# Layer 0 of a feature-interaction tower: products of pairs on VectorE in five of 32 units, in place of sums on TensorE and squares on ScalarE

## The reference: what is computed

```
xk = x0
for W in (W0, W1, W2):
    xk = relu(einsum('bmd,bhd,mhk->bkd', x0, xk, W))   # products of every field with every row of xk
    outs.append(sum(xk, axis=2))                        # over d
z = concatenate(outs, axis=1)                           # (1024, 192)
h = relu(concatenate([z, dense_ctx]) @ W_top1 + b_top1); h = relu(h @ W_top2 + b_top2); y = h @ W_top3
```

## Time and profile before

| | |
|---|---|
| median of 3 runs | 628.99 us (628.71 to 633.98) |
| the profiled execution, its own time | 630.75 us |
| its span, first to last instruction | 629.0 us |
| TensorE / VectorE / GpSimd / ScalarE busy | 606.1 / 514.3 / 444.0 / 322.1 us |
| clock granted to TensorE, mean | 0.997 of full |

### The profile page before, as it was taken

The page is one execution under the profiler, slowest core; times in us unless marked ns, Lnnn a source line. Parts: engine busy times, 40 slices in busy tenths (PEclk is TensorE's granted clock), DMA queues, the critical chain, the costliest instruction groups (busy, mean ns, idle before and its releaser), DMA issues.

```text
span 629.0 us, 8379 instructions
## 1 busy us (share of the span) xinstructions
PE 606.1 (96%) x2884; PEld 210.1 (33%) x2884; DVE 514.3 (82%) x454; ACT 322.1 (51%) x539; POOL 444.0 (71%) x346
## 2 busy tenths in 40 slices
PE   2788999999999999999999999999999999999998
PEld 1522333333333333333333333333333333333354
DVE  0058499999989998999999998999899998888600
ACT  1225546564636465564556463646546455643554
POOL 6777577878787878788787878787887876456400
PEclk9998999999999999999999999999999999999999
DMA  4886877877776768777678777677776767750000
GB/s 128 288 286 219 285 253 259 284 254 281 268 264 215 281 235 266 262 247 259 235 280 282 277 245 256 221 278 266 254 258 248 263 246 279 268 160 35 1 0 1
DMA packets 45199, 144.49 MB, mean 230 GB/s; under 512 B 9619, under 2 KB 24085, under 8 KB 32870
## 3 DMA queue, kind: packets, MB, share of 16 engines
q1 hardware_dynamic: 36966, 141.85, 62.3%
q0 software_dynamic: 8192, 2.11, 3.1%
HBM read 139.21 MB, written 4.72 MB: 229 GB/s over the span
## 4 chain that ended last, share of the span: by engine, by line
PE 95%; ACT 2%; DMA 1%; SPq 1%; DVE 1%; issue 0%; DVEq 0%
PE acc L658 68%; PE acc L650 13%; PE x_ps L624 5%; PE x_ps L691 2%; PE sums_ps L691 2%; PE acc L636 2%; DMA w_sb<-in_w 1%; PE acc L710 1%; ACT x_ps L520 1%; DVE dve_ring L579 1%; PE sums_ps L698 1%; PE acc L638 0%; ACT pair_squares L501 0%; PE sums_ps L705 0%; PE sums_ps L624 0%
## 5 line engine op out<-in xcount | busy, mean ns | idle before, releaser
L579 DVE TENSOR_TENSOR dve_ring<-x_wide,x_ps 128x1024 f32<-128x1024 f32 x428 | 488.2, 1212 | 62.1 <-issue 39.5
L658 PE MATMUL acc<-dve_ring,w_sb 128*64 128x512 f32 x1712 | 492.2, 595 | 5.8 <-DVE dve_ring L579 5.8
L460 POOL DMA_INDIRECT gathered<-in_table,idx x256 | 243.9, 953 | 69.6 <-issue 63.6
L472 POOL TENSOR_TENSOR pool_ring<-x_wide,x_sb 128x1024 f32<-128x1024 f32 x84 | 199.1, 2379 | 81.4 <-ACT x_sb L529 48.3
L658 PEld LDWEIGHTS acc<-dve_ring,w_sb 128*64 128x64 f32 x1712 | 155.1, 137 | 294.7 <-issue 273.4
L650 PE MATMUL acc<-pool_ring,w_sb 128*64 128x512 f32 x336 | 139.5, 592 | 0.0
L636 PE MATMUL acc<-pair_squares,w_sb 128*64 128x512 f32 x256 | 115.7, 592 | 2.4 <-ACT pair_squares L501 2.4
L520 ACT ACTIVATE x_ps<-acc 64x512 f32<-64x512 f32 x128 | 73.0, 570 | 77.9 <-PE acc L658 64.4
L524 ACT ACTIVATE layer_out<-acc 64x512 f32<-64x512 f32 x96 | 56.5, 588 | 60.3 <-PE acc L658 35.8
L501 ACT ACTIVATE pair_squares<-x_ps 128x1024 f32<-128x1024 f32 x32 | 32.8, 1026 | 98.3 <-PE sums_ps L624 98.3
L529 ACT COPY x_sb<-layer_out 64x512 f32<-64x512 f32 x128 | 79.0, 617 | 3.6
(11 more groups left out here) (36 smaller groups left out, 131.3 us busy)
## 6 DMA issues: line engine op xcount, KB each, us to landing
x_wide<-x_rows SPq DMA_DIRECT2D x96, 1024.0 KB, 7.8
x_wide<-x_rows SPq DMA_DIRECT2D x32, 768.0 KB, 5.6
x_wide<-x_rows SPq DMA_DIRECT2D x32, 256.0 KB
gathered<-in_table,idx POOLq DMA_INDIRECT x256, 5.4
x_rows<-gathered SPq DMA_DIRECT2D x32, 128.0 KB, 2.3
w_sb<-in_w SPq DMA_DIRECT2D x2, 512.0 KB, 5.1
x_rows<-gathered SPq DMA_DIRECT2D x32, 16.0 KB, 2.6
x_wide<-in_W_top SPq DMA_DIRECT2D x1, 512.0 KB, 6.4
```

Source lines behind the costliest of these rows:

```text
L460: pool.indirect_dma_start(gathered[:, c, j % 2, e * DIM:(e + 1) * DIM], None, table, bass.IndirectOffsetOnAxis(ap=idx[:, unit, e:e + 1], a ...
L472: nc.gpsimd.tensor_tensor(pool_ring[:, c], x0_step(c, j, layer, 2 * d, 2).rearrange("p (s n) -> p s n", n=COLS), x_sb[:, layer - 1, c, :]. ...
L579: nc.vector.tensor_tensor(dve_ring[:, c, slot:slot + width, :], x0_step(c, j, layer, i, width).rearrange("p (s n) -> p s n", n=COLS), x_ps ...
L658: done = nc.tensor.matmul(a, w, dve_ring[:, c, n % DVE_RING + i - at, :], start=first, stop=last)
```

## The change

Five units, (0, 4), (0, 6), (0, 8), (0, 10) and (0, 12), named `BY_PRODUCTS`, make their layer 0 otherwise. Their `sums` burst and the two squares of it are left out. SP loads a fifth operand for them, the *partners* (128 x 512, 256 KB): partition 4m+q holds field m+4+12q. It lands in the last tile of `pair_squares`. VectorE then multiplies the first four steps of `x0_wide` by the partners in one instruction of 128 x 2048 (`pairs`), both operands in SBUF, and writes the four tiles of `pair_squares`. Those are the products of all pairs. TensorE's five steps of layer 0 stay, with other weights (`w0p_sb`, summed at the start from two arrays, and `w0p_diag`). ScalarE still squares the fields by themselves. For the same five j GpSimd takes one more double of layer 2 of thread 1: doubles 2 and 5 in place of 5 alone.

```diff
+PARTNER, PARTNER_APART = 4, 12
+BY_PRODUCTS = frozenset((0, j) for j in range(4, 14, 2))
...
-    return {1: (6,), 2: ((3, 7), (5,))[c]}[layer]
+    return {1: (6,), 2: ((3, 7), (2, 5) if (0, j) in BY_PRODUCTS else (5,))[c]}[layer]
...
+def pairs_slot(c, j):
+    return begin(c, j) + 6
...
# pe_order
-            works.append((sum_slot(c, j) + 0.5, "sums", c, j + 1, 0, 0))
+            if (c, j + 1) not in BY_PRODUCTS:
+                works.append((sum_slot(c, j) + 0.5, "sums", c, j + 1, 0, 0))
# dve_order
+        if (c, j + 1) in BY_PRODUCTS:
+            works.append((pairs_slot(c, j), "pairs", c, j + 1, 0, 0, 0))
# sp_order
             works.append((at + 30, "block", c, j + 2, 0))
+            if (c, j + 2) in BY_PRODUCTS:
+                works.append((at + 32, "partners", c, j + 2, 0))
             works.append((at + 34, "block", c, j + 2, 1))
...
+            def load_partners(c, j):
+                rows = rows_of(c, j)
+                sp.wait_ge(layer0_done[c], j)
+                sp.dma_start(partner_steps(c),
+                             bass.AP(rows.tensor, rows.offset + PARTNER * COLS,
+                                     [[COLS, FIELDS], [PARTNER_APART * COLS, Q], [1, COLS]])).then_inc(partners_loaded[c], 16)
...
+            sp.dma_start(w0p_sb[:], w0_near).then_inc(pair_weights, 16)
+            sp.dma_start(w0f_sb, w0_far).then_inc(pair_weights, 16)
+            sp.dma_start(w0p_diag[:], w0_diag).then_inc(pair_weights, 16)
...
# GpSimd, ahead of its loop
             pool.wait_ge(w0_summed, 1)
+            pool.wait_ge(w0_added, 2)
...
# ScalarE, squares
+                if (c, j) in BY_PRODUCTS:
+                    act.wait_ge(layer0_done[c], j)
+                else:
+                    act.wait_ge(sums_made, sums_before(c, j) + 4)
                     bank = sum_banks(c, j)
                     nc.scalar.activation(pair_squares[:, c, 0:2, :], x_ps[:, bank:bank + 2, :],
                                          ACT.Square).then_inc(squares_made, 1)
                     nc.scalar.activation(pair_squares[:, c, 2:4, :], sums_ps[:], ACT.Square).then_inc(squares_made, 1)
...
+            def pairs(c, j):
+                wait_first_step(dve, c, j)
+                wait_block(dve, c, j, 0)
+                dve.wait_ge(partners_loaded[c], 16 * (products_before(c, j) + 1))
+                dve.wait_ge(layer0_done[c], j)
+                nc.vector.tensor_tensor(
+                    pair_squares[:, c],
+                    x0_step(c, j, 1, 0, SUM_TILES).rearrange("p (s n) -> p s n", n=COLS),
+                    partner_steps(c).unsqueeze(1).broadcast_to([P, SUM_TILES, COLS]),
+                    ALU.mult).then_inc(pairs_made[c], 1)
...
# VectorE, ahead of its loop
+            dve.wait_ge(pair_weights, 48)
+            nc.vector.tensor_tensor(w0p_sb[:], w0p_sb[:], w0f_sb, ALU.add).then_inc(w0_added, 1)
...
# TensorE, layer0
+                if by_products and i == 0:
+                    pe.wait_ge(pairs_made[c], products_before(c, j) + 1)
+                if by_products and i == SUM_TILES:
+                    pe.wait_ge(squares_made, squares_before(c, j) + 1)
...
-            pe.wait_ge(w0_added, 2)
+            pe.wait_ge(w0_added, 3)
```

More of the change, by code:

```diff
@@ L118, in dve_groups, with squares_before, sums_before, products_before @@
     return [(i, 2) for i in range(0, STEPS, 2) if not by_pool(c, j, layer, i)]
+def pairs_slot(c, j):
+    return begin(c, j) + 6
+def squares_before(c, j):
+    return sum(1 if (d, n) in BY_PRODUCTS else 3 for n in range(j + 1) for d in range(THREADS) if (n, d) < (j, c))
+def sums_before(c, j):
+    return sum(4 * ((d, n) not in BY_PRODUCTS) for n in range(j + 1) for d in range(THREADS) if (n, d) < (j, c))
+def products_before(c, j):
+    return sum((c, n) in BY_PRODUCTS for n in range(j))
+def squares_of_sums(c, j):
+    return 0 if (c, j) in BY_PRODUCTS else squares_before(c, j) + 1
 def mlp_plan():
@@ L230, in cin_tower @@
 def cin_tower(nc, dense_ctx, ids, base, table, w_top1, b_top1, w_top2, b_top2, w_top3,
-              w0_ab, w0_ba, w0_diag, in_pair, of_field, w1, w2, ident, out):
+              w0_ab, w0_ba, w0_diag, w0_near, w0_far, in_pair, of_field, w1, w2, ident, out):
     with ExitStack() as ctx:
@@ L258, in cin_tower @@
         w0d_sb = sb("w0d_sb", [P, HK])
+        w0p_sb = sb("w0p_sb", [P, SUM_TILES, HK])
+        w0p_diag = sb("w0p_diag", [P, HK])
         in_pair_sb = sb("in_pair_sb", [P, P])
@@ L273, in cin_tower @@
         of_field_sb = pool_ring[:, 0, 1, :].rearrange("p (t n) -> p t n", n=P)
+        w0f_sb = pool_ring[:, 1, 1, 0:SUM_TILES * HK].rearrange("p (t k) -> p t k", k=HK)
         dense = pool_ring[:, 1, 0, 0:TILES * DIM].rearrange("p (t f) -> p t f", f=DIM)
@@ L303, in cin_tower @@
         weights_b = sem("weights_b")
+        pair_weights = sem("pair_weights")
         w0_added = sem("w0_added")
@@ L314, in cin_tower @@
         squares_made = sem("squares_made")
+        partners_loaded = sems("partners_loaded")
+        pairs_made = sems("pairs_made")
         dve_made = sems("dve_made")
@@ L430, in _ @@
                     stage(c, j)
+                elif work == "partners":
+                    load_partners(c, j)
                 elif work == "block":
@@ L510, in finish @@
                 wait_layer(act, layer, c, j)
[L512 to L517, removed]
+                if layer == 0 and c == 0 and j > 0 and squares_of_sums(1, j):
+                    act.wait_ge(squares_made, squares_of_sums(1, j))
+                if layer == 0 and c == 1 and 0 < j < UNITS - 1 and squares_of_sums(0, j + 1):
+                    act.wait_ge(squares_made, squares_of_sums(0, j + 1))
+                if layer == 1 and j < UNITS - 1 and (c, j) != (0, 0) and squares_of_sums(c, j + 1):
+                    act.wait_ge(squares_made, squares_of_sums(c, j + 1))
                 if layer < 2:
@@ L601, in _ @@
                     product(c, j, layer, i, width)
+                elif work == "pairs":
+                    pairs(c, j)
                 else:
@@ L628, in layer0 @@
                 a = acc[j % 2][out_half(c), :]
[L629 to L634, removed]
+                if i == 0 and j > 1:
+                    pe.wait_ge(out_made[2][c], j - 1)
+                by_products = (c, j) in BY_PRODUCTS
+                if by_products and i == 0:
+                    pe.wait_ge(pairs_made[c], products_before(c, j) + 1)
+                if by_products and i == SUM_TILES:
+                    pe.wait_ge(squares_made, squares_before(c, j) + 1)
+                if not by_products and i != 1:
+                    pe.wait_ge(squares_made, squares_before(c, j) + (1, 0, 2, 2, 3)[i])
                 if i < SUM_TILES:
-                    nc.tensor.matmul(a, w0_sb[:, i, :], pair_squares[:, c, i, :], start=(i == 0), stop=False)
-                else:
-                    nc.tensor.matmul(a, w0d_sb[:], own_squares[:, c, :],
+                    w = (w0p_sb if by_products else w0_sb)[:, i, :]
+                    nc.tensor.matmul(a, w, pair_squares[:, c, i, :], start=(i == 0), stop=False)
+                else:
+                    w = w0p_diag if by_products else w0d_sb
+                    nc.tensor.matmul(a, w[:], own_squares[:, c, :],
                                      start=False, stop=True).then_inc(layer0_done[c], 1)
@@ L744 @@
         arrays[name] = tiles
+    m, t, q = np.meshgrid(np.arange(FIELDS), np.arange(SUM_TILES), np.arange(Q), indexing="ij")
+    near, far = (m + Q_APART * q + t) % FIELDS, (m + PARTNER + PARTNER_APART * q) % FIELDS
+    twice = ((far - near) % FIELDS == FIELDS // 2) & (near > far)
+    for name, (first, second) in (("w0_near", (near, far)), ("w0_far", (far, near))):
+        tiles = np.where(twice[..., None], np.float32(0), w0[first, second])
+        arrays[name] = tiles.transpose(0, 2, 1, 3).reshape(P, SUM_TILES, HK)
     arrays["of_field"] = np.zeros((P, SUM_TILES, P), np.float32)
```

24 lines of the change are left out of this document (11 added, 13 removed).

## The result

The change makes the kernel slower by 0.6%: 634.45 us as the median of 18 runs (632.27 to 637.00) against 631.03 for the kernel before (628.10 to 633.98, 18 runs), a ratio of 1.0059 with a 95% interval of 1.0040 to 1.0078. That is +3.4 us where -5.4 was forecast, and above the range.

A forecast was written before the change was run, and what follows sets the result against it. TensorE bounds the kernel, VectorE 1.3 to 2.4 us short of it. Five bursts at -1.23 us plus 0.7 given back make -5.4 us: 625.3 for the profiled execution, median 623.6, range 622.5 to 632.

The forecast's parts named there:

- the duration of the pair products: VectorE, 128 x 2048 from SBUF: 2.26 us long, next product 2.16 us after; a second SBUF operand costs nothing by itself.
- the first rival: VectorE's pair products and GpSimd's doubles wait for each other; chance 0.27 for (a), 0.12 for (b).
- case (a): VectorE gets its turn after GpSimd's first double: 1.6 lost against 1.23 gained, sum +1.4, 630.4 us; chance 0.27.
- the sign that its mechanism is wrong: In the profile after, TensorE waiting at all five places; a wait of about 0.7 us was expected at unit (0,4) alone.
- thread 0 half a slot behind thread 1: TensorE's order of steps: (0,9) step 14 taken nine slots after the burst, thread 0 half a slot behind.
- What is removed: TensorE's five bursts of sums, 5 x 1.23 = 6.2 us; the squares on ScalarE give nothing.
- VectorE's leads: VectorE's products behind the pair products: (1,8) step 12 keeps 0.65 us, (0,9) step 14 keeps 0.55, so no stall.
- GpSimd's two doubles: Start at 357.75 behind three gathers, end at 360.1 and 362.5, 0.75 and 0.55 us in hand: costs nothing.
- The first unit: Unit (0,4), VectorE has no double less: products come 2.16 us later, TensorE waits some 0.7 us, given back.
- The additional double: GpSimd's new double runs to 354.1, before TensorE takes step 4 at about 355.7: in time.
- the loads: Partners there by about 356, before 358.55; thread 1's near rows land at 369.2, before its burst at 370.4: nothing.

The follow-up runs named there:

- e1: Changed kernel with the pair products of all five units 5.5 slots later, behind GpSimd's two doubles; 628.38 us, ratio 0.9973 to the kernel before.
- e7: e6 with GpSimd's additional doubles two units earlier, so the first unit with pair products has one ahead too; 624.49 us, ratio 0.9892 to the kernel before.
- e6: e1 with one GpSimd gather moved behind its double for step (1,j,1,12) in the units of the pairs; 624.81 us, ratio 0.9891 to the kernel before.
- e3: Kernel before with only GpSimd's additional double in thread 1's units 4, 6, 8, 10 and 12; 631.02 us, ratio 1.0026 to the kernel before.
- e2: Changed kernel without GpSimd's additional double, pair products at their old slot; 630.96 us, ratio 1.0020 to the kernel before.

## Why the prediction was wrong

**The failed step** is the duration of the pair products. "I take 2.16" was right for the work (2.28 alone; 2.26 was worked out) and wrong for the place: in the change VectorE's next product starts 365.01 - 361.33 = 3.68 us after them. The argument that reads of a second SBUF operand cost nothing rested on a sum of 256 columns which, as the prediction itself says, met no double of GpSimd. It told nothing about the one condition that mattered, and "the rows neither show such a wait nor exclude it" should not have left the forecast ahead of the rival. The Trainium skill, "SBUF — State Buffer", section "Who interferes with whom", says that a VectorE instruction with two SBUF inputs contends with a GpSimd instruction that reads SBUF, and that the one issued later blocks. This case agrees: 1.60 us until the first double ended, 2.2 us for the second until the pair products ended, and neither in e1. That the second SBUF operand is the reason is not tried by itself, since no run moves an operand; what speaks for it is that VectorE's products with one operand in PSUM read the same `x0_wide`, ran beside the same doubles, and never took over 1.24 us in any of these kernels. The rule and the overlap of the two (358.55 inside 357.75 to 360.1, in the prediction's own schedule) were both in hand.

**What happened is the first rival, case (a),** with VectorE's turn between the two doubles. The order of the turns, the steps that wait and the signs were as it drew them, and TensorE waits at all five places, which it had named as the sign that its mechanism is wrong. Its price was too small: 1.6 us lost for each of four units against 2.0 measured. TensorE's wait for (1,8) step 12 is 0.88 where 1.0 was reckoned, the one for GpSimd's second double 0.66 where 0.6 was. Missing was the third part: a step that comes late against its partner of the other thread shifts the pairing, and 0.42 more goes at the next burst. The rows could have told it: the prediction placed thread 0 half a slot behind thread 1, but in the kernel before the two run side by side. Of the two records of line 658 below, the second one, at 363.83, is the first of (1,8) step 12, and the record of line 650 is the first of (0,9) step 12.

```profile
363.41 1.01 PE L658 MATMUL acc<-dve_ring,w_sb 128*64 128x512 f32 x2
363.83 0.59 PE L650 MATMUL acc<-pool_ring,w_sb 128*64 128x512 f32 x1
```

So in the change (0,9) step 12 was due at 366.28, with its partner. It came 1.09 late, and 0.66 + 0.42 + 0.05 = 1.13 is what was lost behind the first wait. For the first unit (a) had a balance of zero, and it is +0.27: the pair products were issued 0.48 us before a double's end, the step behind them came 0.89 late (159.23 in place of 158.34), and 0.60 more went behind it, where the pairs shift as well.

**The sum.** Forecast -5.4, measured +3.4, apart by 8.8: four units give +0.80 in place of -1.23 (8.1) and the first one +0.27 in place of -0.53 (0.8). Another 2 us of the distance from 623.6 to 634.45 is the starting point: the kernel before had a median of 628.99 in the three runs shown and 631.03 in 18.

**Right, by the runs:**
- *What is removed*: 1.23 us a burst. e7 shows 68.40 - 67.18 = 1.22, five times.
- *VectorE's leads*: 0.65 us was to remain for (1,8) step 12 after pair products of 2.16. The product came 0.82 after 365.40; with 2.16 in place of 3.68 it would have had 0.70 in hand.
- *GpSimd's two doubles*, the first one: 0.75 us in hand. In e1, where nothing holds it up, it ends 0.76 ahead of TensorE. The second was to have 0.55 and has 0.15 (360.08 against 360.23), by the same half slot; (0,9) step 14 of VectorE, given 0.55, would by the same correction have had 0.1, which no run tries.
- *The first unit*: e7's 67.18 against e6's 68.27 is that missing double. That it costs something there is right; its size is not tested, for in e6 the pair products stand later and are themselves what TensorE waits for (1.1 lost, where 0.7 was reckoned for the products behind them).
- *The additional double* by itself costs nothing in the loop (e3).

**Not looked at:** GpSimd behind the pair products. This is not why the change lost, where only the first unit's pair products met a gather (2.85 us); it bears on why e1 gained so little. The prediction followed its two doubles and the loads and stopped there. A gather that lasts 2.27 us instead of 0.94 puts everything behind it on GpSimd 1.3 us back; the double for (1,9) step 12, 12 us later, then lacks 0.8. That the long gather is what made it late in e1 is worked out, not tried by itself; what is shown is that 1.25 us more room ends the loss.

## What to carry to other kernels

When a new instruction brings two engines to the same resource for the first time, a short example that met no rival says nothing of its price: lay both engines' instructions on one time axis, and if they overlap, forecast the wait. Such a wait may show only as a longer record, so compare min, median and max of a line before reading its mean. And where TensorE runs two threads in pairs, lateness need not show as idle time: in e1 a double 0.82 us late cost 0.9 us a period, while TensorE was busy all through it with steps that had no partner. So look for records without a partner, and not for gaps alone; moving one instruction of 1.25 us gave the 0.9 back in each of four units.

## What the runs showed of the hardware that was not expected

- VectorE's waiting instruction got its turn between two queued doubles of GpSimd that otherwise run back to back, in all four units where it met the first of them: the second double had started its record at 362.88, before the first one's end, and still came after the pair products.
- Gathers wait too. In the kernel before no gather took over 1.11 us. A gather issued while pair products ran ended 0.8 to 0.9 us after their end in e1 and e2 (363.80 against 362.97; 362.15 against 361.29), and at unit (0,10) so lasted 2.27 and 2.85 us. The one already under way when they started (360.24 in e1) was not held up.
